# Graph attention on one core: the loads of the one-hots for weighing begun three steps ahead instead of two

## The reference

```python
x_i = xl[dst]
x_j = xr[src]
e = jax.nn.leaky_relu(x_i + x_j, NEG_SLOPE)
logit = jnp.einsum('ehc,hc->eh', e, att)
m = jax.ops.segment_max(logit, dst, num_segments=n)
ex = jnp.exp(logit - m[dst])
den = jax.ops.segment_sum(ex, dst, num_segments=n)
alpha = ex / (den[dst] + 1e-16)
out = jax.ops.segment_sum(alpha[..., None] * x_j, dst, num_segments=n)
```

## Time and profile before

| what | value |
|---|---|
| median of three runs | 6526.3 us |
| profiled execution, its own time | 6522.08 us |
| its span, first to last instruction | 6520.3 us |
| mean granted TensorE clock | 0.839 of full speed |
| PE busy / DVE busy | 4622.5 us (71%) / 3864.3 us (59%) |
| POOL busy / ACT busy | 3852.1 us (59%) / 1597.9 us (25%) |
| queue q10, all DMAs that ScalarE issues among them | 208.97 MB, 11.0% of 16 engines |

### The profile page before, as it was taken

How to read it: one execution, slowest core, us unless ns; L and a number is a source line. 1 busy time by engine, 2 the same in 40 slices (tenths; PEclk the granted TensorE clock), 3 DMA queues, 4 the chain that set the end, 5 groups by cost and what they waited for, 6 DMA issues and landing times. The chain is left out here.

```text
span 6520.3 us, 133948 instructions
## 1 busy us (share of the span) xinstructions
PE 4622.5 (71%) x34231; PEld 4074.0 (62%) x34232; DVE 3864.3 (59%) x9164; ACT 1597.9 (25%) x3365; POOL 3852.1 (59%) x3152
## 2 busy tenths in 40 slices
PE   7868874787888747888887477887763656666665
PEld 5765334677777646777776467777762455555554
DVE  8988126666666566666665766666656433333334
ACT  4764110111111111111111111111111144444443
POOL 0000002778787726887877268878780078888884
PEclk9989986898888878988887788888886778778777
DMA  6863441333333323333333233333331122222221
GB/s 160 221 167 117 121 121 49 80 98 98 98 99 97 96 68 80 98 99 99 99 96 96 68 79 98 99 98 97 93 99 43 47 66 66 65 65 65 66 65 46
DMA packets 633590, 600.24 MB, mean 92 GB/s; under 512 B 244880, under 2 KB 571807, under 8 KB 632685
## 3 DMA queue, kind: packets, MB, share of 16 engines
q0 software_dynamic: 250880, 233.27, 15.7%
q10 hardware_dynamic: 229475, 208.97, 11.0%
q1 hardware_dynamic: 153097, 156.30, 9.0%
HBM read 497.47 MB, written 97.37 MB: 91 GB/s over the span
## 5 line engine op out<-in xcount | busy, mean ns | idle before, releaser
L565 POOL DMA_INDIRECT rows<-row_table,now x2280 | 2829.2, 1241 | 1640.8 <-issue 1527.6
L565 POOL DMA_INDIRECT rows<-node_table,now x800 | 989.9, 1237 | 562.9 <-issue 562.9
L977 DVE SCALAR_TENSOR_TENSOR z<-zp,own 125x512 f32<-125x512 f32 x672 | 464.1, 691 | 832.7 <-PE zp L846 828.1
L857 PEld LDWEIGHTS sums<-both,hot 125*125 125x125 f32 x5376 | 773.9, 201 | 186.9 <-issue 125.8
L857 PE MATMUL sums<-both,hot 125*125 125x137 f32 x5376 | 808.7, 297 | 101.6 <-ACT both L739 73.9
L846 PE MATMUL zp<-rows,ident 125*125 x2700 | 819.2, 430 | 70.2 <-SPq L590 68.9
L865 PE MATMUL turn<-xr,ft 125*125 125x132 f32 x6000 | 785.9, 289 | 70.2 <-DVE ft L946 66.1
L843 PE MATMUL zp<-parts,hot_t 125*125 x8100 | 654.7, 234 | 242.3 <-issue 183.6
L865 PEld LDWEIGHTS turn<-xr,ft 125*125 125x125 f32 x6000 | 760.1, 200 | 76.6 <-DVE ft L946 68.9
L843 PEld LDWEIGHTS zp<-parts,hot_t 125*125 125x125 bf16 x8100 | 614.1, 145 | 278.7 <-issue 276.5
L738 ACT CAST hot<-hot 125x500 f32<-125x500 bf16 x672 | 408.7, 608 | 1479.9 <-PE sums L857 751.1
(11 more groups left out here) (454 smaller groups left out, 5575.7 us busy)
## 6 DMA issues: line engine op xcount, KB each, us to landing
hot<-hots ACTq DMA_DIRECT2D x896, 122.1 KB
hot_t<-hots_t ACTq DMA_DIRECT2D x678, 122.1 KB
counts<-pairs SPq DMA_DIRECT2D x55, 685.1 KB
rows<-row_table,now POOLq DMA_INDIRECT x2280, 3.6
spread_slots<-slot_table POOLq DMA_DIRECT2D x56, 488.3 KB, 5.5
hots_t<-hot_t SPq DMA_DIRECT2D x112, 218.8 KB
hots<-hot_dst SPq DMA_DIRECT2D x112, 218.8 KB
pairs<-cells SPq DMA_DIRECT2D x25, 685.1 KB
```

The source lines that it names most:

```text
L565: pool.indirect_dma_start(rows[:, q, j, :], None, table, bass.IndirectOffsetOnAxis(ap=now[:, n, lane + j:lane + j + 1], axis=0)).then_inc( ...
L857: ins = pe.matmul(sums[:, p, 0:ACCW], hot32[:, p, j * P:(j + 1) * P], values[:, p, j, :], start=j == 0, stop=j == HALF - 1)
L977: dve.scalar_tensor_tensor(out=z[:, p, :, :], in0=zp[:, p, :, 0:D], scalar=0.0, in1=rows_of(own_att, HALF), op0=ALU.max, op1=ALU.mult).the ...
```

## The change

`load_hot` is called for step c + 3 instead of c + 2. Ahead of the first weighing three loads are begun instead of two, and the last call in the final four steps is made only once.

```diff
-            for q in range(2):
+            for q in range(3):
                 load_hot(q, q)
             weigh(0)
...
                     widen(c, GROUP * b + i - GROUP, i, q)
                     load_spread(k + 2, (q + 2) % AHEAD)
-                    load_hot(c + 2, (q + 2) % AHEAD)
+                    load_hot(c + 3, (q + 3) % AHEAD)
...
                     widen(c, last // AHEAD + i, i, q)
-                    load_hot(c + 2, (q + 2) % AHEAD)
+                    load_hot(c + 3, (q + 3) % AHEAD)
             for q in range(AHEAD):
                 widen(TEAMS - AHEAD + q, TEAMS // AHEAD - 1, GROUP - 1, q)
-                if q < 2:
-                    load_hot(TEAMS - AHEAD + q + 2, q + 2)
+                if q == 0:
+                    load_hot(TEAMS - 1, AHEAD - 1)
```

## The result

The changed kernel took 6508.08 us (median of 17 runs, 6500.65 to 6518.72) against 6523.78 us for the kernel before beside it (median of 17). The ratio is 0.9977 with an interval of 0.9969 to 0.9984.

The account below looks back on a forecast made before the run. The prediction took POOL's gathers to bound the body and load waits the three tails; 15 us from the tails and 1 us from the body gave 6506 us profiled, 6510 us as median, range 6495 to 6525.

Parts of the forecast that it names:

- The body is bound by the gathers: Attention body: POOL's 760 gathers a layer set 1171 of 1197.5 us, so shorter load waits there buy almost nothing.
- TensorE's 73.9 us: Body, after each softmax: 38 waits of about 1.95 us for L739 at a block's step 0, untouched by the change.
- A tail step of 1.55 us: Tail, 16 steps a layer: a step falls from 1.885 to 1.55 us; 8 steps save 2.7 us a tail.
- The latency bound of 1.26 us: Tail: the step if a load keeps its 3.50 us with three in flight; the lower bound on a step.
- The head start of 2.25 us a tail: Start of each tail: earlier issue lets step 7's load land at 2313.4 instead of 2315.66, saving 2.25 us.
- The sum: Whole kernel: 15 us from three tails and 1 us from the body, 6506 us profiled, 6510 us as median.
- a gain of 1 us: Body, all layers: fewer POOL waits for free quads save 1 us, bounds 0 and 13 us.
- The queue is full already: Tail rival: loads lengthen to 5.4 us, a step stays 1.885 us, gain only 3 to 9 us; chance 0.20.
- Nothing arrives: Tail rival: something besides the load, such as ScalarE's work and the two-buffer sums, holds it; 6520 to 6532 us; chance 0.10.
- The gathers get longer: Body rival: denser loads and VectorE work lengthen gathers by 12 to 44 ns each, 6540 us and more; chance 0.06.
- a floor of 1.39 us: Tail: by the skill's rule a load uses 5 engines, 74% busy, so a step can shrink no lower than 1.39 us.
- Costs at nothing: Before the first weighing and in the steps: the added load's 0.27 us issue is hidden and the moved wait costs nothing.

Follow-up runs that it names:

- e2_body_only: Three loads ahead in the body, two in the written-out tail, whose step 0 begins no load, against the kernel before: ratio 1.0002 (0.9993 to 1.0011).
- e3_body_one: One load ahead in the body, two in the written-out tail, against the kernel before: ratio 1.0643 (1.0623 to 1.0662), 415 us slower.
- the first pair: Profiles of the kernel before and the changed kernel from the main comparison; the changed kernel's profiled execution took 6517.41 us, ratio of the runs 0.9977.
- the second profile: The changed kernel run once more (`r_after`), unaltered, against the kernel before: profile 6492.65 us, median of 11 runs 6510.60, ratio 0.9986.
- e4_tail_four: The changed kernel with its tail written out and four loads ahead there, three in the body, against the kernel before: ratio 0.9968 (0.9957 to 0.9979).
- e7_split_two: Two ahead, tail written out, each tail load split into DMAs of 112 and 13 partitions, against the kernel before: ratio 0.9969, median 6499.82 us.
- e6_unrolled: The kernel before with its tail written out and nothing else, two loads ahead everywhere, against the kernel before: ratio 0.9993 (0.9984 to 1.0002).

## Why the prediction was right, and where it was not

- *The body is bound by the gathers.* Shown on the chips where the kernel before takes some 6520 us: removing all of ScalarE's waits for loads there gave 1.0002 (`e2_body_only`), and cutting the lead to one cost 415 us (`e3_body_one`). It is not a property of the program alone: on the slower chip POOL waited over 500 us for free quads, and the reason fell with it. The time from first to last gather stayed within 7 us of before in each layer, where the prediction had named 5, and 10 as the sign of being wrong.
- *TensorE's 73.9 us belong to the restart after the softmax.* Right: 77.9 us after, with 42 places for 38.
- *A tail step of 1.55 us.* This term was mis-sized. It is 1.29 to 1.33 us. The step that failed is the one that reads 1.48 us for a load out of the earlier trace rows and takes it for the queue's floor, together with the lengthening of a load to 4.3 us. The gap of the earlier trace rows lies between two widenings in the middle of gathers. The lengthening rests on the 2.93 us of step 5 in the earlier trace rows, taken for a load with little else under way; but the load of step 4 was in flight until 3613.80, so it was not alone:

```profile
3612.50 0.27 ACTq L733 DMA_DIRECT2D hot<-hots  x1
...
3613.80 0.61 ACT L738 CAST hot<-hot 125x500 f32<-125x500 bf16 x1 [0.82 <-DMA hot<-hots]
```

  Measured, a load took 3.63 us on average with two in flight and 3.77 with three (steps 7 to 15 of the three tails), so it hardly grew. The latency bound of 1.26 us, the lower end in the prediction, was the right reading, and (3.77 + 0.3) / 3 = 1.36 is near the 1.31 found. TensorE's 1.20 us, named as a limit, lies close below it: without waits for loads a step took 1.24.
- *The head start of 2.25 us a tail.* It was 2.0 in the first tail: step 7 came 11.33 us after step 0 where it had been 13.34; in the other two it was 1.9 and 1.6. In the first, the rest of the 6.7 us, 4.7, is 8 steps of 0.59.
- *The sum.* The tails saved 20.2 us instead of 15, and the runs showed 15.7 and 10. That the forecast of 16 was hit almost exactly is therefore partly luck: a term of the tail was too small by 5 us, and 5 to 10 us were lost elsewhere, which the prediction does not have (it gave the body a gain of 1 us). The 8.3 us by which the bodies were longer in the first pair were not there in the second profile (3664.7 against 3666.5 us for the three bodies of before), but that profile is the shortest of its runs. The run times lean to a cost of the third load in the body of some 4 us and do not show it; on the slower chip a cost of 31 to 37 us is shown.
- *The rivals.* "The queue is full already" fell (1.3 us a step, and 1.24 with four ahead). "Nothing arrives" fell; its chain of widening and sums, put at 1.1 us a step at most, did hold the steps at 1.24 us once the loads no longer did (`e4_tail_four`, `e7_split_two`), with VectorE's weighing and adding in it. "The gathers get longer" did not occur: mean 1244 ns and 1243 in the two profiles, 1241 before. The Trainium skill's rule on the number of engines (from "DMA: Bandwidth & Descriptors", section on why a DMA increments its semaphore by 16) was given with a floor of 1.39 us. The step came out below it, so the floor was too high: the engines' busy time per load, which it takes for fixed, fell from 7.3 to 7.7 us with two ahead to 6.0 with three (steps 7 to 15). The rule itself agrees with these runs: single loads kept 4.8 engines busy, and with 112 + 13 partitions in `e7_split_two` it was 6.2, and a load took over 1 us less.
- *Costs at nothing.* No trace shows a cost of the load ahead of the softmax or of the moved wait, and no run takes them apart from the cost of the body's lead.

## What to carry to other kernels

Long idle times of an engine for its loads say nothing until one sees who waits for that engine in that part of the program; here 438 us of them were free, and the gain lay in the 40 us in three short tails. When loads sit on the path with a fixed number ahead, the step is load time over lead, until the next chain of waits (here 1.24 us) takes over. Before adding a buffer, look whether the load itself is narrow: splitting it was worth as much as two more steps of lead, and did not touch the body, where a deeper lead cost 31 to 37 us on a chip on which the body had no slack.

## What the runs showed of the hardware that was not expected

- A load of 125 partitions x 1000 B took 3.63 us with two in flight and 3.77 with three; as two DMAs of 112 and 13 partitions it took at most 2.42 us. Over 8 us, 4.8 of the 16 DMA engines were busy with the one and 6.2 with the other.
- Two chips can differ by 5.8% on the same kernel (6519.5 and 6900.7 us). Gathers take the same there (1209 to 1212 ns at the median) and so does VectorE (L980: 690 ns, and 691 in `e6_unrolled`), but TensorE's busy time is 3 to 4% longer and its results are taken up later, by 607 to 728 us in sum against 40. The sign of an edit's effect can differ with the chip: three loads ahead in the body cost 31 to 37 us on the one, and on the others no cost is shown.
